# Cross-attention: row maxima turned by one small transposition and carried to their rows by a transfer on SyncE's queue

## The chip, the cores and the metric

The kernel runs on one core of a Trainium2 chip. The metric is the device time of one execution in microseconds (us); less is better. TensorE is called PE here, VectorE DVE, ScalarE ACT, GpSimd POOL and SyncE SP. SP computes nothing: it waits and issues transfers (DMAs).

## The reference

One decoder layer in fp32: self-attention, cross-attention, then a mixture of eight experts. The change is in the cross-attention, for 16 batches of 224 query rows and 750 context rows, 16 heads of 32 columns:

```python
q = (x @ Wq).reshape(B, N, HEADS, hd).transpose(0, 2, 1, 3)
k = (context @ Wk).reshape(B, M, HEADS, hd).transpose(0, 2, 1, 3)
v = (context @ Wv).reshape(B, M, HEADS, hd).transpose(0, 2, 1, 3)
scores = jnp.einsum('bhid,bhjd->bhij', q, k) * scale
scores = jnp.where(context_mask[:, None, None, :], scores, max_neg)
attn = jax.nn.softmax(scores, axis=-1)
out = jnp.einsum('bhij,bhjd->bhid', attn, v)
...
x = x + out @ Wo
```

The softmax needs the maximum of each query row and head. That maximum is what the changed code moves about.

## The kernel before

The program has three stages one behind the other: self-attention, cross-attention, experts. The cross-attention (about 1093 to 2445 us of the span) loops over batches b. Each batch is four groups g of four heads j; a group's number over all batches is t = 4b + g. The work of every engine is written out by hand in the same pattern: for each g and j a first piece, `first_gap(g, j)`, a second piece, `second_gap(g, j)`. A whole batch takes about 83 us.

For head j of group t, PE makes the raw scores (`scores`, L1180) in two halves h of 112 query rows, into the one PSUM tile `psS`. DVE takes the maximum of each half (`maximum`, L1627) into `x_mx`, and only then may PE write the next scores into `psS`. One group later PE makes the scores a second time, transposed and with the maximum already taken off (`shifted`, L1192, three units for each head), ACT takes the exponential (L1462), and PE multiplies with v at the end of the group (`values`, L1205).

Taking the maximum off is part of the matmul `shifted`. The operand `q_st` has 96 rows of queries and three more, 96 to 98: row 96 meets the mask in `k_st`, and rows 96 to 98 must hold, for every query, what is to be added: the negated maximum in two parts, a rounded high part and the low rest, against ones in `k_st`. A unit of maxima is half a group: M0_g holds heads 0 and 1 of group g, M1_g heads 2 and 3 of the group before g. Unit M0_g must be in `q_st` before `shifted` of head 0 in the next group, M1_g before `shifted` of head 2 in group g. There are 128 units in all, 64 of each kind.

Before the change a unit goes this way. PE turns four columns of `x_mx` with four transpositions (`turn_max`, L1170), each spread over all 128 output partitions, so that the values stand on partitions 96 to 98 at once. ACT writes the high part straight into rows 96 to 98 of `q_st` (`high_max`, L1414), DVE the low part (`low_max`, L1633). No transfer is in it.

SP's queue carries everything that has to change partitions: `place_k` copies the key projections of a group into four `k_st` tiles, three or four transfers for each head (L975 to L979), `place_q` the queries (L990, twelve transfers), and `load_ctx` (L941, L942) brings the context, 1125 KB, and the mask of the next batch. The order on SP is that of `body(b, ...)` in the code and SP blocks at each wait, so whatever is behind waits too. `load_ctx(b + 1)` is the first entry of the body of b, right behind `place_k` of b's own first group, and the transfers of group 1 stand behind it.

Of the kernel before, what the change touches and what calls it, by code (L numbers as in the profile page):

```python
# [6 lines left out]
F32 = mybir.dt.float32  # L7
# [9 lines left out]
P = 128  # L17
# [829 lines left out]
def cross_attention(nc, x1, x1n, ctx, cmask, w_o, router_w, cst, x2, rows_w, logits, op):  # L847

    with ExitStack() as outer:
# [9 lines left out]
        with ExitStack() as c:  # L859
# [12 lines left out]
            less = sb(c, "x_less", [P, 1])  # L872
# [12 lines left out]
            gate, filled, zeroed, stored, rw_turned, rw_out, wo_loaded = (  # L885
                sem("x_" + n) for n in ("gate", "filled", "zeroed", "stored", "rw_turned", "rw_out", "wo_loaded"))
            x_loaded, c_loaded, m_loaded, xres_loaded = op.x_loaded, op.c_loaded, op.m_loaded, op.xres_loaded
            pj_full, hi_done, s_full, s_taken, m_high, valid_done = (
                sem("x_" + n) for n in ("pj_full", "hi_done", "s_full", "s_taken", "m_high", "valid_done"))
# [22 lines left out]
            def k_mult(g):  # L912

                return 16 * (4 if g < 2 else 3)

# [12 lines left out]
            with nc.Block() as block:  # L928
                @block.sync
                def _(sp):  # L930
# [29 lines left out]
                    def place_k(t, b, g, units):  # L960

                        for u in units:
                            hold(sp, gate, pj_free[u.bank], u.after)
                        if g == 0:
                            hold(sp, gate, mask_step, 3 * b + 3)
                        if below(t, 1):
                            sp.wait_ge(zeroed, 1)
                        for j in range(4):
# [12 lines left out]
                    def place_q(b, half, units):  # L981

                        for u in units:
                            hold(sp, gate, pj_free[u.bank], u.after)
                        if not below(b, 1):
                            hold(sp, gate, st_full, 48 * b - 24 + 24 * half)
                        for j in range(4):
# [12 lines left out]
                    def body(b, first, last, more):  # L1000
                        t = 4 * b
                        if not last:
                            load_ctx(b + 1)
                        place_k(t + 1, b, 1, [unit_of(b, "K10"), unit_of(b, "K11")])
                        place_q(b, 1, [unit_of(b, "Q2"), unit_of(b, "Q3")])
# [3 lines left out]
                        place_k(t + 2, b, 2, [unit_of(b, "K20"), unit_of(b, "K21")])  # L1009
                        if more:  # L1010
                            load_x(b + 2, unit_of(b, "X1"))
                        place_k(t + 3, b, 3, [unit_of(b, "K30"), unit_of(b, "K31")])
                        if not first:
                            store(b - 1, unit_of(b, "O1"))
                        if not last:
                            place_q(b + 1, 0, [unit_of(b, "Q0"), unit_of(b, "Q1")])
# [1503 lines left out]
```

## Time and profile before

| | |
|---|---|
| time, median of 3 runs | 3777.01 us (3770.28 to 3780.96) |
| time of the profiled execution | 3775.88 us |
| span of the profiled execution (first to last instruction) | 3774.1 us |
| stretch of the cross-attention | 1093 to 2445 us |
| PE busy in that stretch | 1318.04 of 1352 us |
| DVE, ACT, POOL busy there | 897.05, 749.98, 793.19 us |
| granted TensorE clock there | 0.99 of full speed |

An engine's busy time is the union of its instructions. The span and the time differ by 1.8 us, which lie outside the instructions. PE is nearly always busy in the stretch; the others are not.

### The profile page before, as it was taken

The page shows a single profiled execution, that of the slowest core. Times are in us where ns is not written, and L with a number is a line of the kernel's source. Part 1 is how long each engine was busy: PE and PEld are TensorE (multiplying, and loading weights), DVE is VectorE, ACT ScalarE, POOL GpSimd, SP SyncE. Part 2 cuts the span into 40 slices and gives each one's busy share as a digit, 9 for nine tenths or more (in the row PEclk, how much of TensorE's full clock was granted, in tenths as well). Part 3 has the DMA queues.
Part 4 walks back from the last instruction along what each step waited for, and adds up shares of the span by engine and source line. Part 5 has one row for each costly group of instructions (what it writes and reads, how often), then busy time and mean ns, then how long its engine had stood idle before and what let it go on. Part 6 is the DMA issues. An engine that isn't in the chain of part 4 may idle for free. (4 is left out here: it accounts for less than half of the span.)

```text
span 3774.1 us, 84215 instructions
## 1 busy us (share of the span) xinstructions
PE 3639.7 (96%) x28244; PEld 3139.7 (83%) x28244; DVE 2361.0 (63%) x5543; ACT 1731.9 (46%) x4278; POOL 1305.9 (35%) x1388
## 2 busy tenths in 40 slices
PE   8999999999979999999999999849999999999999
PEld 7888888888868888888888888638998899989998
DVE  6888888888846666666666666576433434434343
ACT  4555555555435555555555555413333333333332
POOL 2333333333325656666556566510101101011010
PEclk9999999999989999999999999869999999999999
DMA  4222222222243434444434343223324334234232
GB/s 127 60 54 63 54 63 53 64 53 64 72 122 94 112 106 104 108 116 107 121 96 113 104 108 97 71 68 94 121 82 122 107 98 123 82 118 123 85 108 69
DMA packets 315057, 349.72 MB, mean 93 GB/s; under 512 B 45308, under 2 KB 232036, under 8 KB 314884
## 3 DMA queue, kind: packets, MB, share of 16 engines
q1 hardware_dynamic: 305796, 318.26, 30.7%
q0 software_dynamic: 9088, 29.17, 2.4%
q8 instruction: 106, 1.74, 0.2%
q14 instruction: 67, 0.55, 0.0%
HBM read 183.23 MB, written 38.91 MB: 59 GB/s over the span
## 5 line engine op out<-in xcount | busy, mean ns | idle before, releaser
L1627 DVE TENSOR_REDUCE x_mx<-x_psS 112x1 f32<-112x752 f32 x512 | 479.7, 937 | 382.2 <-PE x_psS L1180 378.6
L2423 DVE TENSOR_TENSOR hid<-e_psU,act_g 128x280 f32<-128x280 f32 x256 | 115.1, 450 | 622.6 <-PE e_psU L34 585.8
L1462 ACT ACTIVATE x_pt<-x_psE 125x448 f32<-125x448 f32 x768 | 389.6, 542 | 227.6 <-PE x_psE L1192 217.7
L1051 POOL TENSOR_TENSOR part<-x_pt 125x448 f32<-125x448 f32 x255 | 292.4, 1147 | 506.0 <-ACT x_pt L1462 497.1
L2049 POOL DMA_INDIRECT out<-ex_y,sidx x40 | 39.8, 995 | 1020.4 <-DVE ex_y L2457 1010.2
L635 POOL TENSOR_TENSOR qks<-qks,cos 128x448 f32<-128x448 f32 x128 | 148.1, 1157 | 657.0 <-DMA qks<-qk 657.0
L1180 PE MATMUL x_psS<-k_st,q_st 97*112 97x376 f32 x1024 | 287.9, 362 | 24.1 <-DMA k_st<-mk 16.3
L32 PE MATMUL e_psG<-ex_hi,g_hi 128*128 128x280 f32 x1024 | 304.2, 297 | 6.7 <-ACT act_g L2208 4.5
L32 PE MATMUL pj<-xT_hi,win_hi 128*128 128x224 f32 x1024 | 302.2, 295 | 4.0 <-PEq L185 3.9
L2208 ACT ACTIVATE act_g<-e_psG 128x280 f32<-128x280 f32 x256 | 103.7, 405 | 426.4 <-PE e_psG L34 412.1
L1053 POOL TENSOR_TENSOR part<-part,x_pt 125x448 f32<-125x448 f32 x255 | 292.3, 1146 | 20.0
L34 PE MATMUL e_psG<-ex_hi,g_lo 128*128 128x280 f32 x1024 | 298.3, 291 | 0.0
L32 PE MATMUL e_psU<-ex_hi,u_hi 128*128 128x280 f32 x1024 | 297.9, 291 | 0.2 <-DVE hid L2423 0.2
L34 PE MATMUL e_psU<-ex_hi,u_lo 128*128 128x280 f32 x1024 | 297.6, 291 | 0.0
L33 PE MATMUL e_psG<-ex_lo,g_hi 128*128 128x280 f32 x1024 | 297.0, 290 | 0.0
L33 PE MATMUL e_psU<-ex_lo,u_hi 128*128 128x280 f32 x1024 | 297.0, 290 | 0.0
L33 PE MATMUL pj<-xT_lo,win_hi 128*128 128x224 f32 x1024 | 282.6, 276 | 0.0
L34 PE MATMUL pj<-xT_hi,win_lo 128*128 128x224 f32 x1024 | 281.7, 275 | 0.0
L1192 PE MATMUL x_psE<-q_st,k_st 99*125 99x224 f32 x1536 | 261.4, 279 | 5.7 <-ACT x_pt L1462 4.3
L1192 PEld LDWEIGHTS x_psE<-q_st,k_st 99*125 99x125 f32 x1536 | 234.9, 190 | 14.6 <-ACT x_pt L1462 11.1
L2212 ACT ACTIVATE hid_hi<-hid 128x280 fp32r<-128x280 f32 (+1 forms) x256 | 107.1, 418 | 283.4 <-DVE hid L2423 266.5
L698 DVE CUSTOM_DVE_ANT_0 pr<-psS,mask 112x112 f32<-112x112 f32 (+1 forms) x512 | 139.4, 328 | 128.7 <-issue 66.7
(305 smaller groups left out, 10890.3 us busy)
## 6 DMA issues: line engine op xcount, KB each, us to landing
k_st<-kT SPq DMA_DIRECT2D x768, 93.8 KB, 2.2
raw_g<-in_L_ffn_wg SPq DMA_DIRECT2D x128, 256.0 KB
raw_u<-in_L_ffn_wu SPq DMA_DIRECT2D x128, 256.0 KB
raw_d<-in_L_ffn_wd SPq DMA_DIRECT2D x128, 256.0 KB
qks<-qk SPq DMA_DIRECT2D x512, 56.0 KB, 2.0
q_st<-qT SPq DMA_DIRECT2D x384, 56.0 KB, 2.0
ctxt<-in_ctx SPq DMA_DIRECT2D x16, 1125.0 KB
xt<-in_x SPq DMA_DIRECT2D x16, 448.0 KB, 3.7
```

The source lines that it names most:

```text
L32: pe.matmul(out, lh, rh, start=first, stop=False)
L33: pe.matmul(out, lh, rl, start=False, stop=False)
L34: return pe.matmul(out, ll, rh, start=False, stop=last)
L635: pool.tensor_tensor(qks[i][:], qks[i][:], cos[:].unsqueeze(1).to_broadcast((P, 2, T)), ALU.mult)
L698: m = dve.tensor_tensor_reduce(pr[par][:, hd, to:to + n], psS[hd][0:HT, to:to + n], mask[:, h, 0:n], -SD ** -0.5, -NEG, ALU.add, ALU.min, ...
L1051: pool.tensor_tensor(part[:], pt[j][:, 0, :], pt[j][:, 1, :], ALU.add).then_inc(parted, 1)
L1053: pool.tensor_tensor(part[:], part[:], pt[j][:, 2, :], ALU.add).then_inc(parted, 1)
L1180: m = pe.matmul(psS[0:HT, s, 0:376], q_st[0:97, head, h * HT:(h + 1) * HT], k_st[4 * (g % 2) + j][0:97, SHALF[s]], start=True, stop=True)
L1192: m = pe.matmul(psE[(j + i) % 2][0:KR, s * T:(s + 1) * T], k_st[4 * (g % 2) + j][0:99, r * KR:(r + 1) * KR], q_st[0:99, 4 * g + j, :], sta ...
L1462: act.activation(pt[j][:, i, :], psE[(j + i) % 2][0:KR, 0:2 * T], ACT.Exp, scale=XD ** -0.5).then_inc(exp_done, 1)
L1627: dve.tensor_reduce(mx[:, j, h:h + 1], psS[0:HT, :, 0:376], AX.XY, ALU.max).then_inc(s_taken, 1)
L2423: dve.tensor_tensor(h[ring][:, halves[s]], psU[:, 0:CH], act_g[i][:, halves[s]], ALU.mult).then_inc(S["mul"], 1)
```

## The change

PE turns a unit with one transposition. DVE prepares it: behind the second maximum of head 2 (and of head 3) it negates the four columns of the unit, writes the high part and then the low part into `m_parts` (`split_max`, two small instructions). PE transposes these eight columns into eight partitions (`turn_max`, one transposition instead of four), ACT copies the eight rows to `m_row` (`out_max`), and SP moves them with one transfer of 2x4x112 elements into rows 97 and 98 of `q_st` (`place_max`), counted by `m_placed`. PE waits for `m_placed` where it waited for the PSUM bank before. `high_max` and `low_max` are gone. PE turns M0_g a little earlier, right behind the first scores of head 3. On SP, `place_k` and `place_q` are cut in two halves (heads 0, 1 and heads 2, 3), and the new transfers stand between them, except M1_0, which stands first behind `load_ctx(b + 1)`.

```diff
+            m_parts, m_row = sb(c, "m_parts", [HT, 2, 8], F32R), sb(c, "m_row", [8, HT], F32R)
...
+                    def place_max(u, g, i):
+
+                        hold(sp, gate, pj_free[u.bank], u.after)
+                        head = 4 * g + 2 * i
+                        sp.dma_start(q_st[97:99, head:head + 2, :].bitcast(F32), m_row[:].bitcast(F32)).then_inc(m_placed, 16)
...
                     def body(b, first, last, more):
                         t = 4 * b
+                        near, far = range(2), range(2, 4)
                         if not last:
                             load_ctx(b + 1)
-                        place_k(t + 1, b, 1, [unit_of(b, "K10"), unit_of(b, "K11")])
+                        if not first:
+                            place_max(unit_of(b, "M1_0"), 3, 1)
+                        k_units = [unit_of(b, "K10"), unit_of(b, "K11")]
+                        place_k(t + 1, b, 1, k_units, near)
+                        place_max(unit_of(b, "M0_0"), 0, 0)
+                        place_k(t + 1, b, 1, k_units, far)
...
                     def turn_max(u, t, i):
 
-                        pe.wait_ge(s_taken, 8 * t + 4 * i + 4)
+                        pe.wait_ge(m_split, 4 * t + 2 * i + 2)
                         o = bank(u)
-                        for n in range(4):
-                            m = pe.transpose(o[:, n * HT:(n + 1) * HT], mx[:, 2 * i + n // 2, n % 2:n % 2 + 1].to_broadcast((HT, P)),
-                                             ident[0:HT, 0:HT])
...
+                        pe.transpose(o[0:8, 0:HT], m_parts[:, i, :].bitcast(F32), ident[0:HT, 0:HT]).then_inc(pj_full, 1)
...
                                 scores(n, g, j, 0)
+                                if j == 3:
+                                    turn_max(U(f"M0_{g}"), n, 0)
                                 if prev:
-                                    if j == 0:
-                                        done(U(f"M0_{gp}") if g else unit_of(b - 1, "M0_3"))
-                                    elif j == 2:
-                                        done(U(f"M1_{g}"))
+                                    if j in (0, 2):
+                                        pe.wait_ge(m_placed, max_placed(n - 1, j // 2))
                                     shifted(n - 1, gp, j, (0, 1))
...
+                    def split_max(t, i):
+
+                        raw = mx[:, 2 * i:2 * i + 2, :]
+                        hi, lo = (m_parts[:, i, k:k + 4].rearrange("p (j h) -> p j h", j=2) for k in (0, 4))
+                        dve.wait_ge(s_taken, 8 * t + 4 * i + 4)
+                        dve.tensor_scalar(hi, raw, -1.0, None, ALU.mult).then_inc(m_split, 1)
+                        dve.wait_ge(m_split, 4 * t + 2 * i + 1)
+                        dve.scalar_tensor_tensor(lo, raw, -1.0, hi.bitcast(F32), ALU.mult, ALU.subtract).then_inc(m_split, 1)
```

The first place is SP's queue at the turn from one batch to the next: the last transfers of `place_k` for the next batch's group 0, then `load_ctx`, then `place_k` for group 1. Before the change SP has this there:

```order
L977 DMA k_st<-kT 32x750
L979 DMA k_st<-mk 1x15x50
L1022 REGISTER_ALU
L1022 COMPARE_AND_BRANCH
L941 DMA ctxt<-in_ctx 125x6x384
L942 DMA mk_70<-in_mask_BxS_bf 128x750
L975 DMA k_st<-kT 32x750
```

And with the change:

```order
L990 DMA k_st<-kT 32x750
L992 DMA k_st<-mk 1x15x50
L1060 REGISTER_ALU
L1060 COMPARE_AND_BRANCH
L947 DMA ctxt<-in_ctx 125x6x384
L948 DMA mk_70<-in_mask_BxS_bf 128x750
L970 DMA q_st<-m_row 2x4x112
L988 DMA k_st<-kT 32x750
```

The transfer `q_st<-m_row` of M1_0 has come between the mask's load and the first key transfer of group 1; another one, of M0_3, now stands between the transfers of heads 1 and 2 a few rows above.

The second place is DVE at heads 2 and 3 of group 3: `x_mx` are the maxima, `x_lnw` and `x_mv` belong to the norm of the router's rows, `x_rz` is the reciprocal of the softmax sums. Before the change:

```order
L1627 TENSOR_REDUCE x_mx<-x_psS 112x1
L1667 BN_AGGR x_mv<-x_stats 112x2 x2
L1669 TENSOR_SCALAR x_lnw<-x_mv 112x2
L1640 RECIPROCAL x_rz<-x_psYZ 128x112
L1627 TENSOR_REDUCE x_mx<-x_psS 112x1
L1646 TENSOR_TENSOR x_yT<-x_psYZ,x_rz 128x224
L1633 SCALAR_TENSOR_TENSOR q_st<-x_pj,x_less,q_st 3x448
L1627 TENSOR_REDUCE x_mx<-x_psS 112x1
```

And with the change:

```order
L1657 TENSOR_REDUCE x_mx<-x_psS 112x1
L1664 TENSOR_SCALAR m_parts<-x_mx 112x4
L1666 SCALAR_TENSOR_TENSOR m_parts<-x_mx,m_parts 112x4
L1699 BN_AGGR x_mv<-x_stats 112x2 x2
L1701 TENSOR_SCALAR x_lnw<-x_mv 112x2
L1672 RECIPROCAL x_rz<-x_psYZ 128x112
L1657 TENSOR_REDUCE x_mx<-x_psS 112x1
L1678 TENSOR_TENSOR x_yT<-x_psYZ,x_rz 128x224
L1657 TENSOR_REDUCE x_mx<-x_psS 112x1
```

Two small instructions have come between the last maximum of head 2 and the first maximum of head 3, and the one of 3x448 elements in front of the last maximum is gone.

## Rows read from the trace of the kernel before

**Rows 1.** The page: busy time of PE, DVE and ACT.

```profile
PE 3639.7 (96%) x28244; PEld 3139.7 (83%) x28244; DVE 2361.0 (63%) x5543; ACT 1731.9 (46%) x4278; POOL 1305.9 (35%) x1388
```

**Rows 2.** Windows (length, PE, PEld, DVE, ACT, POOL, clock, DMA): the stage; two batches.

```profile
1093.00:2445.00 1352.00, 1318.04 (x11214) 1106.41 (x11215) 897.05 (x1303) 749.98 (x1509) 793.19 (x961) 0.99 0.40 105
1761.29:1844.54 83.25, 82.41 (x715) 69.53 (x711) 56.31 (x83) 47.66 (x96) 50.12 (x63) 1.00 0.41 109
1340.66:1427.36 86.70, 84.00 (x714) 71.03 (x710) 56.34 (x83) 47.79 (x96) 50.08 (x63) 0.98 0.40 105
```

**Rows 3.** PE's waits (total us, times, longest): stage; before 1176 us; after.

```profile
PE x_psS L1180 <- DMA k_st<-mk: 16.3, 7, 7.1
PEld x_psS L1180 <- DVE x_mx L1627: 22.7, 70, 1.1
...
PE x_psS L1180 <- DMA k_st<-mk: 12.8, 2, 7.1
...
PE x_psS L1180 <- DMA k_st<-mk: 3.5, 5, 1.9
```

**Rows 4.** Timeline of PE in the batch from 1761.29 us, groups 0 and 3.

```profile
1757.10 0.55 PE L1170 MATMUL x_pj<-ident,x_mx 112*128 112x112 f32 x4
1758.34 0.61 PE L1180 MATMUL x_psS<-k_st,q_st 97*112 97x376 f32 x2 [0.19 <-DVE x_mx L1627]
...
1765.32 0.55 PE L1170 MATMUL x_pj<-ident,x_mx 112*128 112x112 f32 x4
...
1770.65 0.51 PE L1180 MATMUL x_psS<-k_st,q_st 97*112 97x376 f32 x2
1771.00 0.60 PE L1192 MATMUL x_psE<-q_st,k_st 99*125 99x224 f32 x4
...
1775.19 0.55 PE L1170 MATMUL x_pj<-ident,x_mx 112*128 112x112 f32 x4
1775.58 0.55 PE L1104 MATMUL x_pj<-ident,x_xt 112*128 112x112 f32 x4
```

**Rows 5.** Timeline of DVE at heads 2 and 3 of group 3.

```profile
1755.23 0.94 DVE L1627 TENSOR_REDUCE x_mx<-x_psS 112x1 f32<-112x752 f32 x1 [0.36 <-PE x_psS L1180]
1756.09 0.24 DVE L1667 BATCH_NORM_AGGREGATE x_mv<-x_stats 112x2 f32<-112x6 f32 x2
...
1757.42 0.87 DVE L1627 TENSOR_REDUCE x_mx<-x_psS 112x1 f32<-112x752 f32 x1
...
1761.21 0.17 DVE L1672 TENSOR_SCALAR x_lnw<-x_lnw 112x2 int32<-112x2 int32 x1
1761.41 0.56 DVE L1674 TENSOR_SCALAR x_lnw<-x_lnw 112x2 int32<-112x2 int32 x1
```

**Rows 6.** Timeline of SP (start, time to issue) around the context's load.

```profile
1763.41 0.82 SPq L979 DMA_DIRECT2D k_st<-mk  x1
1764.98 0.29 SPq L941 DMA_DIRECT2D ctxt<-in_ctx  x1
1765.46 3.53 SPq L942 DMA_DIRECT2D mk<-in_mask_BxS_bf  x1
1770.61 0.55 SPq L975 DMA_DIRECT2D k_st<-kT  x1
...
1771.84 0.58 SPq L977 DMA_DIRECT2D k_st<-kT  x1
1772.47 0.84 SPq L979 DMA_DIRECT2D k_st<-mk  x1
```

**Rows 7.** DMA issues of 1741.9 to 1764.5 us (count, size, us to landing).

```profile
k_st<-kT SPq DMA_DIRECT2D x12, 93.8 KB, 2.1
q_st<-qT SPq DMA_DIRECT2D x12, 56.0 KB, 2.0
k_st<-mk SPq DMA_DIRECT2D x4, 2.9 KB, 1.9
```

**Rows 8.** DMA issues of 1765.4 to 1769 us, then of 1771.8 to 1773.4 us.

```profile
mk<-in_mask_BxS_bf SPq DMA_DIRECT2D x1, 93.8 KB, 12.8
...
k_st<-kT SPq DMA_DIRECT2D x1, 93.8 KB, 6.5
k_st<-mk SPq DMA_DIRECT2D x1, 2.9 KB, 7.0
```

**Rows 9.** Timeline of PE after its wait at 1115.73 us, and a batch later.

```profile
1115.73 0.97 PE L1180 MATMUL x_psS<-k_st,q_st 97*112 97x376 f32 x2 [7.14 <-DMA k_st<-mk]
1120.07 0.51 PE L1180 MATMUL x_psS<-k_st,q_st 97*112 97x376 f32 x2
...
1193.90 0.60 PE L1180 MATMUL x_psS<-k_st,q_st 97*112 97x376 f32 x2
1196.53 0.51 PE L1180 MATMUL x_psS<-k_st,q_st 97*112 97x376 f32 x2
```

**Rows 10.** Window that holds the end of that wait (columns as in rows 2).

```profile
1112.70:1119.50 6.80, 3.77 (x13) 3.76 (x14) 1.47 (x2) 0.98 (x2) 0.00 (x0) 0.50 0.50 136
```

**Rows 11.** Groups of the removed steps, and a small ACT copy.

```profile
L1414 ACT ACTIVATE q_st<-x_pj,ident 3x448 fp32r<-3x448 f32 x128 | 91.8, 718 | 8.9 <-PE x_pj L1170 6.0
L1633 DVE SCALAR_TENSOR_TENSOR q_st<-x_pj,x_less,q_st 3x448 fp32r<-3x448 f32 x128 | 88.7, 693 | 68.2 <-ACT q_st L1414 66.1
L1453 ACT ACTIVATE obias_logits<-x_pj 112x16 f32 x13 | 2.4, 184 | 0.3
```

More of the change, by code:

```diff
@@ L914, in k_mult, with max_placed @@
                 return 16 * (4 if g < 2 else 3)
+            def max_placed(t, i):
+                return 32 * t + 16 * i + 16
+            fills = [ones[:]] + [k[96:99, :].bitcast(F32) for k in k_st]
             def placed(b, g):
@@ L979, in place_k, with place_q @@
                                 sp.dma_start(slot[96:97, :].bitcast(F32), mk[96:97, :]).then_inc(k_placed[j], 16)
[L981 to L987, printed above, removed]
+                    def place_q(b, half, units, heads=range(4)):
+                        if 0 in heads:
+                            for u in units:
+                                hold(sp, gate, pj_free[u.bank], u.after)
+                            if not below(b, 1):
+                                hold(sp, gate, st_full, 48 * b - 24 + 24 * half)
+                        for j in heads:
                             rows = slice(32 * j, 32 * j + 32)
@@ L1246, in first_gap @@
                         def first_gap(g, j):
-                            n, nxt, ng = t + g, not (last and g == 3), (g + 1) % 4
+                            nxt, ng = not (last and g == 3), (g + 1) % 4
                             if j < 2 and nxt:
@@ L1513, in second_gap @@
                         def second_gap(g, j):
-                            gp, prev = (g + 3) % 4, not (first and g == 0)
                             if j == 0:
@@ L1522, in second_gap @@
                                     out_v(U("V00"), 0, 0)
-                                if prev:
-                                    high_max(U(f"M1_{g}"), gp, 1)
+                                if not (first and g == 0):
+                                    out_max(U(f"M1_{g}"), t + g - 1, 1)
                             elif j == 1:
@@ L1576, in _ @@
                     n = 4 * B
-                    exps(n - 1, 0, range(3))
-                    high_max(unit_of(B - 1, "M1_4"), 3, 1)
-                    for j in range(1, 4):
+                    out_max(unit_of(B - 1, "M1_4"), n - 1, 1)
+                    for j in range(4):
                         exps(n - 1, j, range(3))
@@ L1694, in first_gap @@
                         def first_gap(g, j):
-                            n, prev, pprev, gp = t + g, not (first and g == 0), not (first and g < 2), (g + 3) % 4
+                            n, pprev = t + g, not (first and g < 2)
                             if j == 0:
```

98 lines of the change are left out of this document (52 added, 46 removed).

## The prediction

> **What bounds the kernel now.** I read the page first: PE is busy 96% of the span, DVE 63%, ACT 46% [rows 1]. Then the windows: the change touches the cross-attention alone, and there PE is busy 1318 of 1352 us at full clock; a steady batch lasts 83.25 us, of which PE works 82.41 [rows 2]. So the stage is as long as PE's list of work plus what PE waits. Whatever is taken off DVE or ACT is worth something only where PE waits for them, and every new wait of PE counts in full. The table of waits shows two that matter: PE waited seven times, 16.3 us in all, for a key transfer behind the context's load, and its weight loads 70 times, 22.7 us, for a maximum of DVE [rows 3]. These 22.7 us are gaps of the weight loader, which runs ahead of the matmuls, so most of them are no time of PE; but they say where DVE stands directly in front of PE.
>
> **The PE work that goes.** Four transpositions start at 1775.19 and the next instruction at 1775.58, 0.39 us, so three fewer save 0.29 us a unit [rows 4]. 128 units give 37 us at most. It must be asked for each kind whether PE's time is the limit right behind it.
>
> M1 units (64) are turned behind head 0, ahead of projections that fill PE. There the saving counts: 64 x 0.29 = **-18.6 us**.
>
> M0 units (64) are turned between the two scores of head 3. The second scores wait until DVE has taken the first scores' maximum. In group 3 that maximum starts at 1757.42, takes 0.87 us and the scores start at 1758.34 with a wait for it [rows 4, 5]. DVE came there by an unbroken chain from the maximum at 1755.23 [rows 5]. PE is therefore not the limit at that point, and turning faster only lengthens its wait. I give these units no gain.
>
> **What DVE gets.** `split_max` lies in that very chain. A DVE instruction of 112x2 takes 0.17 us and the one that depends on it starts 0.20 us after it began [rows 5]. Two such are 0.40 us, plus the overlap of 0.08 that the next instruction had with the maximum (1755.23 + 0.94 against 1756.09 [rows 5]). I take 0.40 us per group as a mean over the four groups, between 0.3 (where PE arrives a little after DVE) and 0.48. 64 x 0.40 = **+25.6 us**. The bounds for all M0 units together are -18.6 us (PE were the limit after all and DVE's two instructions hidden) and +31.
>
> The `low_max` that goes, 0.69 us of DVE in front of the last maximum, and the `high_max`, 0.72 us of ACT [rows 11], are worth almost nothing. What waits behind that maximum is the first scores of the next group, and PE works through `values` meanwhile. The new ACT copy of 8x112 is nearest to the one of 112x16, 0.18 us [rows 11]; it is hidden where its predecessor was.
>
> **The transfers.** Each unit now also needs SP and the queue. In a quiet stretch a transfer lands 1.9 to 2.1 us after its issue begins, small or large [rows 7], and SP spends about 0.6 to 0.8 us to issue one [rows 6]. PE, ACT and SP's wake-up add about 0.7. From turning to use there are therefore some 3 us. M0_g has the second scores of head 3 and `values` in between, M1_g the rest of head 0 and all of head 1: for M1_0 the turn is at 1765.32 and the use at 1771.00, 5.7 us [rows 4]. In a quiet queue the transfers of the other seven units of a batch are hidden, with 1 to 3 us to spare. In the queue order their predecessors are key or query transfers that take SP 6 us per half; I followed SP through a batch with these costs, and M1_1 and M0_3 are the closest. I take 0 for them, with an upper bound of 1 us each per batch.
>
> M1_0 is different. It stands right behind `load_ctx(b + 1)`. In the steady batch the context's load is issued at 1764.98, the mask's load at 1765.46, and SP is held until 1768.99 by it; that load lands 12.8 us after its issue began, at 1778.3 [rows 6, 8]. PE needs M1_0 at 1771.00. So the question is whether a small transfer issued at about 1769.1 lands 2 us later or only when the loads have passed. The transfers that followed answer it: of those issued between 1771.8 and 1773.4 a key transfer took 6.5 us and one of 2.9 KB took 7.0 us, against 2.1 and 1.9 in the quiet stretch [rows 7, 8]. They were issued at 1771.84 and 1772.47 [rows 6], so they landed at 1778.3 and 1779.5. A transfer of little size does not pass the load.
>
> The Trainium skill says why (DMA: Bandwidth & Descriptors, "Why a DMA increments its semaphore by 16 and not by 1"): a transfer from SP runs on the largest number of engines up to 16 that divides the slowest dimension of both sides, and on the lowest-numbered ones, each working its ring in order. By that the context's load (125 partitions) runs on engines 0 to 4, the new transfer (8 rows to 2) on engines 0 and 1, both of them loaded. If its engines were other ones, the sum would be that of the second case below; no row of this trace tells which engines a transfer used.
>
> The wait, step by step, in the steady batch: the mask's load lands at 1778.3; SP now has one more transfer (M0_3) ahead of the load, +0.65; DVE's longer chain in group 3 delays the batch's own start against SP's list, -0.45; the small transfer itself, +0.2. It lands at 1778.7. PE gets there 0.29 earlier, at 1770.7. The wait is **8.0 us**. Bounds: 0.6 (issued at 1769.2, landing 2.1 later) and 9 (landing 1.0 later, with the last of the small ones). It happens where there is both an M1_0 and a load: batches 1 to 14, 14 times: **+112 us**.
>
> **The clock.** After a wait of 7.14 us PE's clock is at 0.50 of full (1.2 GHz) in the window 1112.7 to 1119.5 [rows 9, 10], and the step from one scores to the next took 4.34 us where it takes 2.63 a batch later [rows 9]. That is 1.7 us. The new wait is 8 us; bounds 0 and 3.4 (half of 6.8 us). I take 2.0, less 0.5 because the slower PE reaches head 3 later and DVE's longer chain there costs nothing in that group: 14 x 1.5 = **+21 us**.
>
> The Trainium skill (TensorE: Matmul & The Clock Gate, "HAM oscillation — how this bites in real kernels") warns of just this pattern, a wait for a transfer that lets the clock fall at every turn of a loop. The trace agrees with one instance, the window at 0.50 after 7.14 us.
>
> **What the new wait swallows.** Behind the load PE now waits at the start of group 1 for keys. Of the 16.3 us, 12.8 lie before 1176 us, in batch 0, which has no M1_0; the other 3.5 us [rows 3], and the clock's fall with the longest of them (the batch of 86.70 against 83.25 us [rows 2]), some 5 us, are covered: **-5 us**. The last batch ends with two transfers in sequence, where little hides them: **+1 us**.
>
> **Sum:** -18.6 + 25.6 + 112 + 21 - 5 + 1 = +136 us. The profiled execution took 3775.9 us (span 3774.1 and 1.8 around it), 1.1 below the median of the runs. 3775.9 + 136 = **3912 us**.
>
> **The rivals.**
>
> The case above, that M1_0 lands behind the loads, 0.82. Its own range goes from 14 x (6.5 + 0.5) plus a few (3870) to 14 x (9 + 3) (3945).
>
> Second, the transfer passes the loads (it runs where they don't): the wait is 0.6 us, no fall of the clock, the seven transfers hidden. 14 x 0.6 - 18.6 + 25.6 = +15, with 1 us each at one close unit per batch +31: 3791 to 3807 (slower, but two in eight of it within 11 us if DVE's term is smaller), 0.08. Against it stand the 7.0 us of a 2.9 KB transfer [rows 8].
>
> Third, on the other side: the transfer passes and PE was the limit behind M0 after all, DVE's chain having room. Then 128 x 0.29 = -37 us, plus the 0.6: 3739 to 3748, 0.04. Its place is the second scores of head 3; it decides where the added DVE time is under 0.05 us, and the wait shown there [rows 4] speaks against it. The point from which the change gains at all is a wait of M1_0 below 0.5 us with DVE's term zero: 14 x w < 37 gives w < 2.6 us; by rows 8 it is 8.
>
> Fourth, worse: other units' transfers come late too, because SP, held at M0_0 until group 0's last head, runs behind with group 1's far keys and the queries (M1_1), or the clock stays low longer. One more wait of 2 to 3 us per batch: 3945 to 3975, 0.06.
>
> **Chances and range.** About 0.3% (11 us) is what a measurement of this kernel can tell from no change. Faster 0.04 (third case), same 0.02, slower 0.94 (the rest). The range 3860 to 3948 holds the first case and a little of the fourth.
>
> **What would show it.** In the profile after: a wait of PE at `shifted` (x_psE) for the transfer q_st<-m_row, 14 times, 7 to 9 us each; batches of about 93 us; a short fall of the clock after each; that transfer in the list of issues with a median near 2 us but 9 to 10 us for those behind the load; no wait for k_st<-mk in group 1 after batch 0; DVE's and ACT's busy time smaller by 40 to 70 us without gain. Wrong would make it: M1_0 landing 2 us after its issue, a load that is over sooner when the key transfers come later, or PE not held by DVE at head 3.

## The result

The changed kernel takes 3947.62 us (median of 5 runs, 3945.63 to 3949.77); the kernel before, beside it, 3777.01 us (5 runs, 3770.28 to 3783.06). The ratio is **1.0454, 95% interval 1.0439 to 1.047**: 171 us slower, where the sum said 136 slower. That is the very end of the range of 3860 to 3948 us: the median lies 0.4 us inside it, and the ratio a hair past it (3948 / 3777.01 is 1.0453).

The page of the changed kernel, busy time over the whole span, against [rows 1]. DVE's busy time is the same (2361.6 against 2361.0), which the prediction had smaller by 40 to 70 us; ACT has 71 us less. PE has 48 us more though it has 384 matmul records less: the clock.

```profile
PE 3687.6 (93%) x27860; PEld 3140.6 (80%) x27860; DVE 2361.6 (60%) x5671; ACT 1661.3 (42%) x4278; POOL 1302.6 (33%) x1386
```

Windows of the changed kernel with the columns of [rows 2]: the stage, a steady batch, and 6.8 us around the end of one wait (at 1957.93). The first window ends about 21 us behind the stage: the last scores start at 2596.8 us, in the kernel before at 2422.7.

```profile
1093.00:2640.00 1547.00, 1374.84 (x10872) 1114.55 (x10872) 911.19 (x1471) 684.64 (x1519) 791.51 (x961) 0.93 0.36 94
1923.00:2018.54 95.54, 86.85 (x688) 71.23 (x687) 56.52 (x91) 43.28 (x97) 49.98 (x62) 0.93 0.36 96
1955.82:1962.62 6.80, 4.69 (x21) 4.69 (x22) 0.51 (x1) 1.91 (x4) 0.52 (x1) 0.50 0.27 75
```

A batch grew from 83.25 us to 95.5, at a mean granted clock of 0.93 instead of 1.00. In the third window it is 0.50, which is 1.2 GHz of 2.4. PE's waits in the stage, against [rows 3] (us in total, times, longest):

```profile
PE x_psE L1225 <- DMA q_st<-m_row: 86.1, 14, 8.0
PE x_pj L1147 <- DVE cT L1639: 21.8, 15, 1.5
PE x_psS L1213 <- DVE x_mx L1657: 16.1, 20, 1.1
PE x_psS L1213 <- DMA k_st<-mk: 12.4, 2, 6.8
PE x_psE L1225 <- ACT x_pt L1494: 12.1, 28, 0.6
```

The first row is the wait that was forecast: 14 times, for the new transfer. The second was in no list of mine: PE's transposition of the context waits 1.5 us in every batch for DVE's `cT`, an operation that the diff doesn't touch (3.7 us in all before the change, 15 times).

To see where a batch grew I took the starts of the 32 first halves of `scores` in each batch, their distances, and the median of each distance over batches 5 to 13. A step is named by the scores at which it begins, group.head.half. The batches are counted from 0; the steady one of the windows, from 1923, spans the end of batch 8 and most of batch 9, which begins at 1942.74. The steps that carry the difference, and the sum of all 32 (us):

```
step                           before   after    difference
0.2.0  M1_0's wait               2.07    9.97    +7.90
0.2.1 and 0.3.0  behind it       3.47    4.31    +0.84
1.3.0                            1.84    2.09    +0.24
2.2.1  cT late                   2.36    3.59    +1.23
3.3.0  maximum late              2.12    3.35    +1.23
3.3.1  clock at 0.50             2.94    4.62    +1.68
0.0.1, 1.0.1, 2.0.1, 3.0.1       9.64    8.75    -0.89   (M1's shorter turns)
all 32                          83.31   95.36   +12.05
```

So there are three parts: 8.7 us of waiting for M1_0 and its clock, 4.4 us behind DVE in groups 1 to 3 (0.24 + 1.23 + 1.23 + 1.68), and 0.9 us saved. The other steps give back 0.2. One piece of the first part may belong to the second: of the 0.84 us, 0.39 is step 0.3.0, and experiment 2, in which nothing waits for M1_0, has 0.38 there too.

**The wait.** Timeline of PE in the batch from 1942.74 us: the turn of M1_0, the last scores before the wait, and the first `shifted` behind it. Then SP's timeline of the same place (start, time to issue), against [rows 4] and [rows 6].

```profile
1946.78 0.26 PE L1205 MATMUL x_pj<-ident,m_parts 112*8 112x112 f32 x1
...
1951.97 0.51 PE L1213 MATMUL x_psS<-k_st,q_st 97*112 97x376 f32 x2
1957.93 1.18 PE L1225 MATMUL x_psE<-q_st,k_st 99*125 99x224 f32 x4 [5.45 <-DMA q_st<-m_row]
```

```profile
1944.97 0.29 SPq L947 DMA_DIRECT2D ctxt<-in_ctx  x1
1945.46 4.20 SPq L948 DMA_DIRECT2D mk<-in_mask_BxS_bf  x1
1949.88 0.75 SPq L970 DMA_DIRECT2D q_st<-m_row  x1
1951.79 0.58 SPq L988 DMA_DIRECT2D k_st<-kT  x1
```

The transfer of 3.5 KB is issued 3.1 us after its turn, because SP is held by the mask's load for 4.2 us. It lands 8 us later. The trace also holds the times at which the transfers count up their semaphores. (The context's load and M1_0 have one more each, shortly after their issue, at 1945.43 and 1951.04, which is left out here.)

```
context load   5 increments: 1956.97 1957.14 1957.25 1957.39 1957.61
mask load     11 by 1952.56, then 1957.20 1957.49 1957.54 1957.65 1957.87
M1_0           2 increments: 1957.40 1957.81
```

The context's load counts up five times as it ends, so I take it to have run in five parts, on five rings; the mask's load had eleven parts done by 1952.56, and the other five are done only as the context's load ends. M1_0 has two parts, and both land in the same microsecond. The Trainium skill (DMA: Bandwidth & Descriptors, "Why a DMA increments its semaphore by 16 and not by 1") gives 5 for 125 rows and 2 for the 8-to-2 transfer, on the lowest-numbered engines; the trace agrees on the numbers, 5 and 2. Which engines they were, no run here shows.

**DVE.** Timelines of DVE, GpSimd and PE at the end of group 3, two batches earlier (against [rows 5]).

```profile
1837.42 0.94 DVE L1657 TENSOR_REDUCE x_mx<-x_psS 112x1 f32<-112x752 f32 x1 [0.36 <-PE x_psS L1213]
1838.28 0.65 DVE L1664 TENSOR_SCALAR m_parts<-x_mx 112x4 fp32r<-112x4 f32 x1
1838.97 0.16 DVE L1666 SCALAR_TENSOR_TENSOR m_parts<-x_mx,m_parts 112x4 fp32r<-112x4 f32 x1
...
1839.47 0.70 DVE L1701 TENSOR_SCALAR x_lnw<-x_mv 112x2 f32<-112x2 f32 x1
```

```profile
1837.76 1.14 POOL L1087 TENSOR_TENSOR part<-x_pt 125x448 f32<-125x448 f32 x1 [0.99 <-ACT x_pt L1494]
1838.98 1.15 POOL L1089 TENSOR_TENSOR part<-part,x_pt 125x448 f32<-125x448 f32 x1
```

```profile
1841.77 0.60 PE L1213 MATMUL x_psS<-k_st,q_st 97*112 97x376 f32 x2 [0.82 <-DVE x_mx L1657]
```

The first instruction of `split_max`, four numbers on each of 112 partitions, takes 0.65 us: it ends at 1838.93, and GpSimd's addition ended at 1838.90. L1701, with two numbers on each, ends at 1840.17, and GpSimd's next addition at 1840.13. The same in group 2, where the full length shows, and where PE's transposition of the context stands behind it:

```profile
1815.99 1.09 DVE L1664 TENSOR_SCALAR m_parts<-x_mx 112x4 fp32r<-112x4 f32 x1
1817.12 0.16 DVE L1666 SCALAR_TENSOR_TENSOR m_parts<-x_mx,m_parts 112x4 fp32r<-112x4 f32 x1
1817.21 1.01 DVE L1639 TENSOR_TENSOR cT<-x_pj,cT 128x375 fp32r<-128x375 f32 x2
```

```profile
1815.92 1.13 POOL L1087 TENSOR_TENSOR part<-x_pt 125x448 f32<-125x448 f32 x1 [2.21 <-ACT x_pt L1494]
```

```profile
1817.91 0.51 PE L1147 MATMUL x_pj<-ident,ctxt 125*128 125x125 f32 x3 [1.48 <-DVE cT L1639]
```

The clock at this place: in batch 8 the same two waits of PE stand before a fall to 0.50 at 1938.76, and 3.3.1 takes 4.62 us.

```profile
1936.83 0.48 PE L1225 MATMUL x_psE<-q_st,k_st 99*125 99x224 f32 x2 [0.42 <-ACT x_pt L1494]
1938.12 0.60 PE L1213 MATMUL x_psS<-k_st,q_st 97*112 97x376 f32 x2 [0.81 <-DVE x_mx L1657]
```

It fell here at the end of 13 of the batches 1 to 14. In batch 7, whose lines stand above (0.82 us before 1841.77), it did not, and 3.3.1 took 2.93 us as before the change. So the late maximum goes ahead of the fall and doesn't always bring it.

All of them together, one row for each instruction of `split_max` (shortest, median and longest in ns):

```profile
L1664 DVE TENSOR_SCALAR m_parts<-x_mx x128: 158/478/1151, 1105.9 to 2598.7; 112x4 fp32r<-112x4 f32 x128
L1666 DVE SCALAR_TENSOR_TENSOR m_parts<-x_mx,m_parts x128: 161/163/1159, 1106.1 to 2599.9; 112x4 fp32r<-112x4 f32 x128
```

The theory that the experiments test: the loss is (1) the wait of M1_0 behind the load, with its clock, and (2) DVE's first small instruction, which waits until the GpSimd instruction under way is done, with the clock's fall that often comes behind the later maximum.

### The profile page after: what moved, and what is told of

The parts are those of the page before. It is cut to its first block and busy times, and to the rows that moved or that the text cites. A ratio compares the mean times of both kernels' runs of the same rounds, so it can differ in the third digit from the quotient of the medians.

```text
span 3946.6 us, 84052 instructions
## 1 busy us (share of the span) xinstructions
PE 3687.6 (93%) x27860; PEld 3140.6 (80%) x27860; DVE 2361.6 (60%) x5671; ACT 1661.3 (42%) x4278; POOL 1302.6 (33%) x1386
## 5 line engine op out<-in xcount | busy, mean ns | idle before, releaser
L1225 PE MATMUL x_psE<-q_st,k_st 99*125 99x224 f32 x1536 | 279.8, 292 | 99.1 <-DMA q_st<-m_row 86.1
```

The lines of the kernel that those rows point to most:

```text
L1225: m = pe.matmul(psE[(j + i) % 2][0:KR, s * T:(s + 1) * T], k_st[4 * (g % 2) + j][0:99, r * KR:(r + 1) * KR], q_st[0:99, 4 * g + j, :], sta ...
```

## The experiments

Ratios are to the kernel before, with their 95% intervals; "a batch" is the sum of the 32 medians, before 83.31 us and after 95.36.

**1. Another form for the first small instruction.** The changed kernel, with two operands from SBUF instead of one.

```diff
-                        dve.tensor_scalar(hi, raw, -1.0, None, ALU.mult).then_inc(m_split, 1)
+                        dve.scalar_tensor_tensor(hi, raw, -2.0, raw, ALU.mult, ALU.add).then_inc(m_split, 1)
```

> The changed kernel with one instruction of split_max in another form: the high part is made as (-2 x maximum) + maximum by an instruction with two tensor operands, in place of the one with one operand and a constant. In the changed kernel that one took 0.48 us in the median and up to 1.15 us for 112x4 elements, its neighbour with two operands 0.16 us. Theory A (the one-operand form is what is slow, and its excess sits in front of the second scores of head 3): the pair takes 0.35 us again, the steps of PE behind head 2 in groups 2 and 3 shrink by 0.7 to 1.2 us each and the falls of the clock at group 3 go: 3890 to 3915 us. Rival B (the time is that of any small DVE instruction there, which waits for its semaphore): 3940 to 3950 us, the first instruction still takes 0.5 us. The wait for M1_0 stays, 14 times, 6 us or a little more.

3948.19 us (3942.93 to 3951.85), 1.0448 [1.0431, 1.0465]: nothing gained. The instruction is as long as before:

```profile
L1664 DVE SCALAR_TENSOR_TENSOR m_parts<-x_mx x128: 152/456/1087, 1104.0 to 2598.7; 112x4 fp32r<-112x4 f32 x128
```

The form is not the remedy. The second instruction of `split_max` is of this same form and mostly short (median 163 ns, longest 1159); in the timelines above it begins just when GpSimd's instruction has ended. The Trainium skill (SBUF — State Buffer, "SBUF: two separate sides") says that DVE and GpSimd share a pair of ports which one holds for its whole instruction while the other is blocked, and names both kinds, a DVE instruction in a fast two-port mode and one with two SBUF inputs beside a GpSimd instruction that reads SBUF. The trace agrees with medians of 456 and 478 ns, and with ends 0.03 us behind GpSimd's: in the changed kernel 124 of the 126 first instructions that began beside a GpSimd instruction ended 0.02 to 0.17 us after it.

**2. The load behind M1_0.** `load_ctx(b + 1)` stands behind `place_max` of M1_0 on SP.

```diff
+                        if not first:
+                            place_max(unit_of(b, "M1_0"), 3, 1)
                         if not last:
                             load_ctx(b + 1)
-                        if not first:
-                            place_max(unit_of(b, "M1_0"), 3, 1)
```

> The changed kernel with load_ctx(b + 1) placed behind the transfer of M1_0 instead of ahead of it. Theory A (a transfer lands only behind those issued ahead of it on SP's queue): the 14 waits of 5.5 to 8 us at the shifted scores go; the load lands some 3 us later than now, so the keys of group 1 are waited for by 1 to 2.5 us; 3855 to 3885 us. Rival B (M1_0 is late because SP itself or the chain PE, ACT, SP takes long at that place): a wait of 3 us or more at the shifted scores stays and the time is 3900 us or more.

3882.73 us (3880.14 to 3890.07), 1.0276 [1.0259, 1.0293]; a batch 91.47. The wait for M1_0 is gone, but the load then covers the keys of group 1:

```profile
PE x_psS L1213 <- DMA k_st<-mk: 45.6, 16, 7.0
```

Step 0.3.1 grew by 2.31 us and 1.0.0 by 1.65. Of M1_0's 8.7 us a batch, 4 came back as another wait: the transfers that stand behind the load on this queue are late in its place.

**3. M1_0 issued by ACT.** ACT copies M1_0 and issues its transfer itself; all else is the changed kernel.

```diff
-                        if not first:
-                            place_max(unit_of(b, "M1_0"), 3, 1)
...
+                    def send_max(u, g, i):
+
+                        act.wait_ge(pj_free[u.bank], u.after)
+                        head = 4 * g + 2 * i
+                        act.dma_start(q_st[97:99, head:head + 2, :].bitcast(F32), m_row[:].bitcast(F32)).then_inc(m_placed, 16)
...
+                                    if g == 0:
+                                        send_max(U("M1_0"), 3, 1)
```

> The changed kernel with the transfer of M1_0 alone issued by ScalarE (behind its copy to m_row) instead of SyncE; the loads stay where they are. Theory A (it is the order on the queue that holds the transfer back): from the other queue it lands about 2 us after its issue while the load is under way, the 14 waits go, 3830 to 3865 us. Rival B (the DMA engines that the transfer needs are busy with the load, whatever the queue): it lands within 1 us of the mask's load as now, waits of 5 us and more stay, 3940 us or more. In between if the engines share themselves out in larger pieces: waits of 1 to 3 us, 3870 to 3910.

3854.92 us (3853.02 to 3856.8), 1.0206 [1.0189, 1.0223]; a batch 88.34. Timelines of ACT, SP and PE in the batch from 1973 us:

```profile
1977.76 0.63 ACTq L1452 DMA_DIRECT2D q_st<-m_row  x1
```

```profile
1975.25 0.29 SPq L947 DMA_DIRECT2D ctxt<-in_ctx  x1
1975.73 3.89 SPq L948 DMA_DIRECT2D mk<-in_mask_BxS_bf  x1
```

```profile
1983.31 0.70 PE L1223 MATMUL x_psE<-q_st,k_st 99*125 99x224 f32 x4 [0.61 <-DMA q_st<-m_row]
```

M1_0 is issued 2.5 us behind the context's load and lands at 1983.19, 5.4 us later, while the context's load ends at 1988.55. So a transfer on another queue does pass the load on its way, but it takes 5.4 us and not the 1.8 that the other transfers of maxima take (median in the changed kernel; 1.7 to 2.1 for all but one, in batch 0). Of the 171 us, 93 (3947.62 - 3854.92) hang on M1_0's place in SP's queue.

**4. The split alone.** The kernel before, in which DVE also executes `split_max` at the changed kernel's places, and nobody uses its result. No transfer is added, and PE still turns four columns.

```diff
+                        dve.tensor_scalar(hi, raw, -1.0, None, ALU.mult).then_inc(m_split, 1)
+                        dve.wait_ge(m_split, 4 * t + 2 * i + 1)
+                        dve.scalar_tensor_tensor(lo, raw, -1.0, hi.bitcast(F32), ALU.mult, ALU.subtract).then_inc(m_split, 1)
...
+                                split_max(n, 0)
...
+                                split_max(n, 1)
```

> The kernel before with split_max added to VectorE at the same places and nothing else (its result is used by nobody; all other work is that of the kernel before). Theory A (two thirds of what the prediction missed is VectorE's added chain with the slow one-operand instruction): 3815 to 3850 us, the waits of PE for a maximum and for the context's low part grow by 30 us or more. Rival B (VectorE's addition is worth what was forecast, 0.4 us a group): 3795 to 3808 us. Rival C (hidden): 3777 within 11 us.

3854.73 us (3850.43 to 3854.89), 1.0204 [1.0187, 1.0221]; a batch 88.86. The same two steps appear as in the changed kernel (2.2.1 +1.23, 3.3.0 +1.23), with 1.5 us of clock at 3.3.1, and 1.27 at 0.3.0. First its small instruction, then its waits of PE in the stage:

```profile
L1636 DVE TENSOR_SCALAR m_parts<-x_mx x128: 159/409/1082, 1104.9 to 2499.0; 112x4 fp32r<-112x4 f32 x128
```

```profile
PE x_psS L1182 <- DVE x_mx L1629: 26.1, 33, 1.4
PE x_pj L1113 <- DVE cT L1611: 21.8, 15, 1.5
```

Two instructions of 0.16 us each, twice in a group, cost 77 us where 25.6 were forecast. Sorted by what GpSimd does when the first of them begins: with a GpSimd instruction under way (87 of 128) the median is 612 ns, with GpSimd idle (41) 170 ns. Of the 87, 85 end 0.02 to 0.16 us after that GpSimd instruction. The second instruction is held up too: 50 of 128 take 0.5 us or more.

**5. The split alone, with GpSimd out of the way.** Experiment 4, with GpSimd's three additions for each head cut to 8, 8 and 4 columns. The sums of the softmax are therefore left out.

```diff
-                            pool.tensor_tensor(part[:], pt[j][:, 0, :], pt[j][:, 1, :], ALU.add).then_inc(parted, 1)
+                            pool.tensor_tensor(part[:, 0:8], pt[j][:, 0, 0:8], pt[j][:, 1, 0:8], ALU.add).then_inc(parted, 1)
...
```

> The kernel before with split_max added (as in the run of split_max alone, 3855 us) and with GpSimd's three additions for each head cut to 8, 8 and 4 columns: the softmax sums then are those of a constant, so this part of the computation is left out; all other engines do the same work. Theory A (split_max waits for GpSimd's instruction under way): its first instruction takes 0.17 us everywhere, and the time falls to 3785 to 3812 us. Rival B (the wait is VectorE's own, for its preceding instruction): 0.5 us in the median as before and 3845 us or more.

3780.91 us (3776.09 to 3781.71), 1.0016 [1.0005, 1.0026]; a batch 84.10.

```profile
L1637 DVE TENSOR_SCALAR m_parts<-x_mx x128: 158/169/172, 1105.0 to 2432.6; 112x4 fp32r<-112x4 f32 x128
```

```profile
PE x_psS L1183 <- DVE x_mx L1630: 11.0, 27, 1.1
PE x_pj L1114 <- DVE cT L1612: 8.2, 15, 0.6
```

All 128 now take 158 to 172 ns. The steps are +0.31, +0.30 and +0.21 at 0.3.0, 2.2.1 and 3.3.0, as the two instructions' own length would have it, and 3.3.1 is back (-0.01): without the longer wait the clock does not fall there in any of the batches 1 to 14. This is the run that shows the cause of the second part: the same instructions in the same places cost 77 us (0.0204 x 3777) with GpSimd's additions and 6 (0.0016 x 3777) without them. The kernel before with only GpSimd's additions cut was not run; but all other steps of the batch are within 0.08 us of the kernel before, so the smaller additions gained nothing elsewhere that could hide a cost.

**6. The split behind the turn.** PE turns four raw columns, ACT writes the high part from PSUM and DVE the low part; each unit then needs two transfers. `split_max` is gone.

```diff
+                        for k in range(2):
+                            sp.dma_start(q_st[97 + k:98 + k, head:head + 2, :].bitcast(F32), m_row[:, k, :].bitcast(F32)).then_inc(m_placed, 16)
...
-                        pe.transpose(o[0:8, 0:HT], m_parts[:, i, :].bitcast(F32), ident[0:HT, 0:HT]).then_inc(pj_full, 1)
+                        pe.transpose(o[0:4, 0:HT], mx[:, 2 * i:2 * i + 2, :].rearrange("p j h -> p (j h)"), ident[0:HT, 0:HT]).then_inc(pj_full, 1)
...
```

> The changed kernel with the split moved behind the transposition: PE turns the four columns of maxima as they are (one transposition, 4x112), ScalarE writes the negated high part of 4x112, VectorE the low part from PSUM and the high part, where low_max was before; split_max is gone, and the two parts go to rows 97 and 98 in a transfer each, so SP issues 256 instead of 128. Theory A (split_max waits for GpSimd's instruction to end, since its operands lie in SBUF alone, and stands ahead of the second scores of head 3): without it groups 0, 2 and 3 lose 1.2 us each less and the fall of the clock at group 3 goes, some 5 us a batch; the waits for M1_0 stay and grow by 0.7 each: 3865 to 3895 us. Rival B (the change's other parts, the earlier turn of M0 or ACT's copy, make PE wait at head 3): 3920 us or more.

4002.85 us (3997.44 to 4005.93), 1.0616 [1.0598, 1.0634], slower than the change. Theory A's gain did not come; the time is in rival B's range, but not for B's reason, since DVE's steps in groups 2 and 3 are back at their old length. It is that the second transfer and its later start make other units late:

```profile
PE x_psE L1226 <- DMA q_st<-m_row: 204.9, 48, 10.2
```

M0_3 costs 2.73 us in each batch, M1_1 2.11 and M1_0 11.66. In the changed kernel these seven other units showed no wait; a second transfer for each, begun after two engines instead of one, is enough to bring out two of them. Which of the two it is, the second transfer or the later start, no run here separates.

**7. The same, with the context's load on more rings.** The load is cut into 120 and 5 partitions.

```diff
-                        sp.dma_start(ctxt[:], at(cv, b, "o p k d -> (o p) k d")).then_inc(c_loaded, 16)
+                        view = at(cv, b, "o p k d -> (o p) k d")
+                        sp.dma_start(ctxt[0:120], view[0:120]).then_inc(c_loaded, 16)
+                        sp.dma_start(ctxt[120:KR], view[120:KR]).then_inc(c_loaded, 16)
```

> Both together: the split behind the transposition and the context's load in 120 and 5 partitions, all transfers where the change has them. If the wait for M1_0 and split_max are the whole loss, the transpositions saved are left: 3735 to 3765 us, faster than the kernel before by 12 us or more. If something third costs, 3775 us or more.

3951.57 us (3948.36 to 3954.55), 1.0477 [1.0459, 1.0494]. It wins back 51 us of experiment 6, and the waits stay about as many (147.7 us, 47 times): those for M1_0 fall from 136.3 to 79.8 us, while M0_3 and M1_1 wait as before (+2.75 and +2.14 us a batch). The narrow load was a part of the first; the other two don't hang on it.

**8. The changed kernel with that wider load.**

> The changed kernel with the context's load cut in two transfers, 120 partitions and 5, in the same place ahead of M1_0. Theory A (a transfer of 125 partitions is carried by 5 of the 16 DMA engines, in about 10 us, and M1_0 needs two of these five; 120 partitions go over 15): the load is over 4 to 6 us after its issue, the mask's load lands some 6 us after its issue instead of 13, and M1_0 is waited for by less than 1 us: 3830 to 3865 us. Rival B (the load takes what 1125 KB take, whatever its cut): landing and waits as now, 3940 us or more.

3879.02 us (3875.31 to 3881.95), 1.0282 [1.0265, 1.0299]; a batch 91.92. PE's waits, and SP's time to issue the mask's load (shortest, median, longest in ns):

```profile
PE x_psE L1227 <- DMA q_st<-m_row: 45.4, 15, 4.2
```

```profile
L950 SPq DMA_DIRECT2D mk<-in_mask_BxS_bf x15: 363/369/369, 1100.9 to 2364.5; - x15
```

The mask's load is issued in 0.37 us instead of 3.8, and lands after 8.5 us instead of 12.6. M1_0's wait fell from 6 us a batch to 3. It still waits for the load that is ahead of it: in batch 8 it lands at 1824.04, and the last count of the context's load is at 1823.99. Only a part of the gain is M1_0's. Against the changed kernel step 0.2.0 is 2.21 us shorter, but 0.2.1 is 0.91 longer; 3.3.1 is 1.68 shorter, since the clock fell at the end of group 3 in only 6 of the batches 1 to 14 (in 13 in the changed kernel), although 3.3.0 is as late as ever (3.35 us). The same late maximum comes with a fall in one batch and without one in the next, and what decides it is not shown.

**9. The wider load alone, in the kernel before.**

> The kernel before with the context's load cut in 120 and 5 partitions and nothing else, as the measure for the two runs beside it. The waits for keys behind the load (3.5 us behind batch 0, 12.8 in it) shrink: 3762 to 3775 us; 3777 if the load was no cost there.

**3769.43 us (3766.05 to 3774.43, 12 runs), 0.9982 [0.9974, 0.9991].** It is the fastest of all kernels here, by less than the 0.3% that one comparison can tell, but with twelve runs the interval excludes 1. A batch is 83.22 us against 83.31: the gain is not in the steady batches. Of the 7.4 us between the spans, 5.5 are in two batches, the first (80.65 instead of 82.63 us) and the one with the clock's fall of [rows 2] (83.23 instead of 86.70). The landing of the mask's load, median of the six in 1800 to 2300 us, is:

```profile
mk<-in_mask_BxS_bf SPq DMA_DIRECT2D x6, 93.8 KB, 8.4
```

**10. Both cures: ACT's issue, wider load.** The whole computation.

> The changed kernel with the whole computation, M1_0's transfer issued by ACT, and the context loaded as 120 and 5 partitions. It asks whether the two cures of M1_0 add up, or whether the load on more rings takes back what ACT's early issue gave. Theory A (they don't add up; what is left is DVE's split beside GpSimd and the clock's falls of group 3, which neither cure touches): a steady batch is that of the kernel with small GpSimd additions, 84.25 us, plus what the whole additions cost in the kernel that only splits (88.86 - 84.10 = 4.8), so 88.3 to 89.1 us; M1_0 waits 0.7 to 1.5 us in each batch; time 3852 to 3872, no faster than with ACT's issue alone (3854.92). Rival B (each takes its part, the wait of M1_0 is gone and with it a clock fall): a batch of 86.5 to 87.5, time 3825 to 3845.

3884.01 us (3882.72 to 3888.79), 1.0297 [1.0283, 1.0311]; a batch 90.57. They don't add up, and it is 29 us slower than ACT's issue alone, which is outside what either theory said:

```profile
PE x_psE L1225 <- DMA q_st<-m_row: 35.6, 15, 3.7
```

From ACT's issue to the landing M1_0 took 6.4 to 8.6 us (batches 5 to 13) where it took 4.8 to 5.6 with the narrow load. In batch 10 it lands at 2001.38, and the last count of the context's load is at 2001.14; with the narrow load it landed 5.4 us before the load's end (experiment 3). Why a load on more rings delays a two-part transfer on another queue more is not shown; the mask's load, whose issue takes 3.5 us less there, may be what it meets, but that is only a guess.

**11. Both cures, and GpSimd out of the way.** As 10, with the additions of experiment 5; the softmax's sums are left out.

> The changed kernel with M1_0's transfer issued by ScalarE, the context's load in 120 and 5 partitions, and GpSimd's three additions for each head cut to 8, 8 and 4 columns (the softmax sums are then those of a constant: this part of the computation is left out). If the wait behind the load and split_max's wait for GpSimd are the whole loss, what is left is the M1 transpositions saved (0.86 us a batch measured so far), split_max at its bare 0.35 us in each group (0.8 us a batch in the run of split_max alone with GpSimd idle) and some tenths at M1_0: 3762 to 3785 us. If a third cost of 1 us or more per batch is left, 3795 us or more.

3806.3 us (3805.84 to 3812.34), 1.0085 [1.0069, 1.01]; a batch 84.25: +1.25 us for M1_0, +0.38, +0.30 and +0.22 for the split, -0.89 for M1's turns. In two batches (90.37 and 90.13 us long, the steady ones 84.2) M1_0's wait was 4.0 and 4.4 us, and the clock fell for 6.8 us behind it. So even with both causes nearly gone the layout doesn't reach the kernel before, and my 3762 to 3785 us was too low. By the steps no third cause is needed in a steady batch: 1.25 of M1_0 and 0.90 of the split's bare length, less 0.89, are more than the +0.94 of the batch. Some 6 us of the difference lie behind the cross-attention, and I have not traced them.

**12. The split later.** The whole computation; `split_max` of M0 behind the first maximum of head 3, M0 turned behind the second scores of head 3, M1_0 and M0_3 issued by ACT, wider load.

> A version meant to be faster than both kernels: the whole computation, with split_max of M0 behind the first maximum of head 3 and its transposition behind the second scores of head 3, the transfers of M1_0 and M0_3 issued by ScalarE, and the context's load in 120 and 5 partitions. Theory: the chain in front of the second scores of head 3 is as before the change, so its 4 to 5 us a batch go; M0_3 comes later, and costs up to 1.5 us a batch at head 0: 3760 to 3800 us. Rival: M0_3 is late by 2.5 us and the clock falls there, 3810 us or more.

3889.4 us (3888.43 to 3896.32), 1.0304 [1.029, 1.0318].

```profile
PE x_psE L1222 <- DMA q_st<-m_row: 55.3, 30, 3.8
```

The maximum of head 3 is no longer late (3.3.0 +0.00), but four other steps grew: 0.2.0 +2.91, 1.2.0 +1.40, 2.3.1 +1.59 and 3.3.1 +2.08. The first two are waits for transfers (M1_0 14 times, M1_1 15 times). In 2.3.1 no transfer is waited for: PE waits twice for DVE's `cT`, 0.55 and 0.87 us, where it waited 0.15 before. In 3.3.1 PE waits nowhere for more than 0.2 us; the step takes about 3.4 us without and 5.0 to 5.1 with a fall of the clock, which came in 6 of the batches 1 to 14, in batch 6 behind waits of 0.42 and 0.19 us only. So of the two places tried for the split, one makes the maximum of head 3 late, and with the other `cT` and M1_1 come later.

## Why the prediction was right in its direction and short in its size

**M1_0's wait: right in mechanism, place and count.** 14 waits, each until the load's last parts land. The trace shows 86.1 us in 14 waits: two of 8.0 us, in batches 1 and 8, and twelve of 3.5 to 6.9. The difference goes with the clock's fall at the end of the batch before, which the forecast didn't have. Where it was absent (batches 0 and 7), the context's load was issued 3.8 or 3.9 us after the next batch began, as in the kernel before (3.7), and the wait was the 8.0 us of the forecast. Where it came, it held PE back and not SP: the load was issued 0.5 to 2.5 us after the batch began, and the wait for M1_0 was shorter by 1.1 us or more. Experiment 8 shows the same, waits of 1.2 to 2.4 us behind a fall and 3.4 to 4.2 without. The two losses are therefore not independent: much of what the fall costs in group 3, M1_0's wait gives back. With what follows at the slow clock the step is 8.74 us a batch, and 8.0 + 1.5 was forecast: 122 us against 133. The rival in which the transfer passes the load is false on SP's queue (experiment 3 shows that it is half true on another).

**M1's turns: right.** 0.9 us a batch against 1.16. **M0's turns, no gain: right.** They stand in the steps 0.3.0 to 3.3.0, and in experiment 6, which has the single transposition but no `split_max`, these four are +0.06, +0.01, 0.00 and 0.00. (The remark that the change gains at all "below 0.5 us" of M1_0's wait doesn't fit its own sum, 37 / 14 = 2.6 us.)

**DVE's term failed, in "two such are 0.40 us".** I priced each new instruction by the 0.17 us of one neighbour [rows 5]. The row below it in the same group, of the same shape, showed 0.56, and I passed over it. It ended at 1761.97; the trace of the kernel before has GpSimd there, until 1761.96:

```profile
1761.29 0.67 POOL L1057 TENSOR_TENSOR ptsum<-part 125x224 f32<-125x224 f32 x1
```

Experiment 4 prices the term, with the clock's fall behind it, at 77 us and not 25.6; with GpSimd out of the way (experiment 5) the steps are 0.2 to 0.3 us, at the low end of what I had taken and below it. The term also had the wrong place: I looked only at PE behind `scores` of head 3, while in group 2 the loser is `cT`, 1.23 us a batch.

**The clock's term was put in one place only.** I charged it behind M1_0's wait. It also fell at the end of group 3 in 13 batches, after two idle pieces of PE of 0.42 and 0.82 us, and cost 1.68 us there (22 us in all). In batch 7 the same two pieces stand without a fall; why, stays open. I had used the clock's fall in the other direction, as something that makes DVE's chain cheaper.

**What the wait swallows: small and right in sign.** The waits for k_st<-mk fell from 16.3 us to 12.4 [rows 3].

Summed over all batches of the two traces, the steps give +122.4 us for M1_0's wait with its clock, +62.9 for the four steps behind DVE, -13.2 for M1's turns and +1.6 for all others: +173.7 us; the spans differ by 172.5 (3946.6 - 3774.1). From 136 to 174 it is +37 for DVE and the clock behind it (62.9 against 25.6), -11 for M1_0's wait with its clock (122.4 against 133), +5 for M1's turns and +6 for what was taken as swallowed (1.6 against -4).

## What to carry over

A transfer that replaces work of an engine is placed in a queue: find out which large transfer is ahead of it and when that one's last part lands, for this is when the small one lands. An instruction of a few numbers is not free where its engine stands in a chain: read all neighbours of its shape in the timeline and not the shortest, lay GpSimd's timeline beside them, and follow every engine that waits behind. Look at the granted clock in every place where a change adds idle pieces, the small ones too, and count in how many batches it falls. Where one loss delays PE ahead of a wait for a queue that isn't delayed, the second loss shrinks by it: don't add the two.

## What the runs showed of the hardware

- A DVE instruction of 112x4 from SBUF to SBUF takes 0.16 to 0.17 us alone and up to 1.15 us when a GpSimd addition is under way; it mostly ends 0.03 us after that one. With GpSimd's additions cut down, 128 of 128 took 158 to 172 ns.
- The granted clock fell to 0.50 for 3.4 us after idle pieces of only 0.42 and 0.81 us, one behind the other (at 1938.76 in the changed kernel), and did not fall after the same pieces a batch earlier (1840.48 and 1841.77), nor in 8 of the batches 1 to 14 of experiment 8.
- A transfer of 3.5 KB behind a load of 1125 KB landed 7.9 to 9.6 us after its issue on the load's own queue, 4.8 to 5.6 us on ACT's; all but one of the other transfers of that size in the changed kernel took 1.7 to 2.1 us.
- The context's load as 120 and 5 partitions instead of 125: the mask's load behind it landed 8.4 us after its issue and not 12.9, and held SP for 0.37 us and not 3.8.
